# A row write of a direction in four transfers instead of six, and a signal for each of the two kinds of rows

## Chip, cores and metric

One core of one Trainium2 chip. The metric is the device time of one execution of the whole program, in microseconds; the kernel runs one program on that core.

## The reference

The model is a small vision tower on 32 images of 96 x 96: patches to tokens, a state-space layer, a mixture of 8 experts (top 2), then a second layer with a two-directional Mamba block and another top-2 mixture. There are 38 tokens an image and 192 features. The change lies in how the two scans get their inputs. They compute, cut to the core:

```python
# layer 0, per token: features Dm=192, states N=16
dA = jnp.exp(a[:, None, :] * dt[None, :, None])
cur = u_t[:, :, None] * (b[:, None, :] * dt[None, :, None])
state = (dlt[:, :, None] * state + (1.0 - dlt[:, :, None]) * cur) * dA
y = jnp.sum(state * c[:, None, :], axis=2) + u_t * D_param

# layer 1, for each of two directions: features DI=192, states NS=16
dt = jax.nn.softplus(dt @ dt_W + dt_b)
dA = jnp.exp(dt_t[:, :, None] * A)
h = dA * h + (dt_t * u_t)[:, :, None] * B_t[:, None, :]
y = (h * C_t[:, None, :]).sum(-1)
```

## The kernel before, in words

The 32 images are worked on in 4 groups of 8 images, T = 304 tokens each. Features lie on the partitions: the first 128 in one piece, the last 64 packed, so that a row block of 128 partitions and PK = 304 + 152 columns holds all of them: columns 0 to 303 are features 0 to 127, columns 304 to 455 hold features 128 to 191, with the first half of the tokens on partitions 0 to 63 and the second half on partitions 64 to 127.

A scan wants another layout: 16 states x 8 features on the partitions. So each direction of a group writes two kinds of rows to DRAM (rows_d, 2 x 2 x 192 x 304): kind 0 is DL, the steps (in the first pass the deltas), kind 1 is WV, the steps times the input. Each of the 12 steps of a scan (QSTEPS, 16 features each) reads its share of both kinds back, each feature's row broadcast to 16 partitions, into one of 4 slots of a ring (dA and BB, fill_slot, line 470).

The program has three parts. The first pass (layer 0's scan, line 505 on for SyncE) goes through the groups; the experts follow (lines 507 to 551); the second pass does, for each group, direction 0 (part_a) and direction 1 (part_b) of the Mamba block, with the tail of the group before and the input of the group after written by hand between the 12 steps of each part. Each engine's order is written out: its function for a part runs n = 0 to 11 and places each piece of work at a given n.

What the prediction's steps touch:

- SyncE issues all the row transfers. `write_first_rows` (line 462) writes a group's rows in the first pass, six transfers, after the signal P.w_ready. `write_rows` (line 579) does it in the second pass, six transfers, after Q.w_ready, which is signalled by the memset at line 1258. For direction 1 it is called ahead of the read of step 11 of direction 0; for direction 0 of the next group, after the last read of direction 1. `read_rows` (line 590) waits until the scan four steps before has freed the slot. `rows_there` (line 587) waits until all the writes of a direction have landed. After the write for the next group stands `read_gates` (line 601), three reads of the gates of the group before, and only then `rows_there` and the reads of direction 0 of the next group.
- VectorE's `steps` (line 1243) makes the rows: five operations on 128 x 456 numbers (lines 1249 to 1254), each of which waits for the one before through the signal PREP.chain, then a memset of one token of each image of DL to RESTART (1e16), so that the scan starts anew there. It is placed at n = 6 of part_a for direction 1 and at n = 7 of part_b for direction 0 of the next group. `direction_step` (line 1189) multiplies the next step's BB by B (line 1186) and scans (line 1200). `gated_output` (line 1260) takes the sum of the direction before, at n = 1.
- ScalarE takes the exponential of the dA rows two steps ahead (`q_decay`, line 864), and waits for Q.w_ready before it overwrites the buffer LZ (line 859). In the first pass `delta` (line 899) waits for the writes of the group before.
- GpSimd multiplies the scan's result by C (line 725), and the mixture's inputs by the gates (line 733).
- TensorE sums over the states (line 1641), takes the gated output (`direction_out`, line 1625), and does the products of the mixture, spread over the steps around the turn from one group to the next; line 1514 is the helper that issues all its products. `add_mixture` (line 1425) on VectorE waits for them.

Of the kernel before, what the change touches and what calls it, by code (L numbers as in the profile page):

```python
# [9 lines left out]
T = IMG * SEQ  # L10
# [95 lines left out]
def vit_tower(nc, x_p, c128a, c64a, c128, c64, ex_m, ex_r, ex_b, out_m, out_r):  # L106
    fp32, bf16, i32, u32 = mybir.dt.float32, mybir.dt.bfloat16, mybir.dt.int32, mybir.dt.uint32
    ALU, ACT, AX = mybir.AluOpType, mybir.ActivationFunctionType, mybir.AxisListType
    with ExitStack() as ctx:
# [211 lines left out]
        P.w_ready, Q.w_ready, base_ready = sig("p_w_ready", 1), sig("q_w_ready", 2), sig("base_ready", 1)  # L321

# [5 lines left out]
        P.rows_written, rows_written = both_passes("rows_written", 96)  # L328
# [10 lines left out]
        PREP.chain, NORM.chain = sig("prep_chain", 10), sig("norm_chain", 2)  # L339
# [108 lines left out]
        def _(sp):  # L448
# [12 lines left out]

            def write_first_rows(p):

                sp.wait_ge(P.w_ready.sem, P.w_ready.after(p, 1))
                for kind, x in enumerate((P.DL, P.WV)):
                    sp.dma_start(rows_d[p % 2, kind, 0:DM, :], x[:, 0:T]).then_inc(P.rows_written.sem, 16)
                    sp.dma_start(rows_d[p % 2, kind, DM:D, 0:HALF], x[0:DR, T:PK]).then_inc(P.rows_written.sem, 16)
                    sp.dma_start(rows_d[p % 2, kind, DM:D, HALF:T], x[DR:128, T:PK]).then_inc(P.rows_written.sem, 16)
# [17 lines left out]
            def first(s, p, m):  # L486
                if s is not None:
                    sp.wait_ge(P.rows_written.sem, P.rows_written.after(s, 96))
                for c in range(QSTEPS):
                    if c == 5:  # L490
                        if m is not None:
                            sp.wait_ge(scan_out.sem, scan_out.after(m, 1))
                            sp.dma_start(h_md[m], M.Hm[:, :]).then_inc(h_stored.sem, 16)
                            sp.dma_start(h_rd[m], M.Hr[:, :]).then_inc(h_stored.sem, 16)
                        if follows(p) is not None:
                            sp.wait_ge(tok_mm.sem, tok_mm.after(p, 2))
                            sp.dma_start(xp[:, :, :], x_p[p + 1]).then_inc(s_x, 16)
                    if c == QSTEPS - 1 and p is not None:
                        write_first_rows(p)
                    if s is not None:  # L500
                        read_first_rows(s, c)
                    if s == 0 and c >= SLOTS:
                        sp.dma_start(zeros[:, c - SLOTS, :], ZERO).then_inc(s_zero, 16)
# [75 lines left out]
            def write_rows(g, k):  # L579

                sp.wait_ge(Q.w_ready.sem, Q.w_ready.after(g, k + 1))
                for kind, x in enumerate((DIRS[k].DL, DIRS[k].WV)):
                    sp.dma_start(rows_d[k, kind, 0:DM, :], x[:, 0:T]).then_inc(rows_written.sem, 16)
                    sp.dma_start(rows_d[k, kind, DM:D, 0:HALF], x[0:DR, T:PK]).then_inc(rows_written.sem, 16)
                    sp.dma_start(rows_d[k, kind, DM:D, HALF:T], x[DR:128, T:PK]).then_inc(rows_written.sem, 16)

            def rows_there(g, k):
                sp.wait_ge(rows_written.sem, rows_written.after(g, 96 * (k + 1)))
# [169 lines left out]
        def _(act):  # L758
# [140 lines left out]
            def delta(s, p):  # L899
                act.wait_ge(delta_mm.sem, delta_mm.after(p, 1))  # L900
                if s is not None:
                    act.wait_ge(P.rows_written.sem, P.rows_written.after(s, 96))
# [139 lines left out]
        def _(dve):  # L1042
# [200 lines left out]
            def steps(g, k):  # L1243

                s = DIRS[k]
                links[PREP] = 5 * k
# [7 lines left out]
                link(PREP, g, nc.vector.tensor_tensor(s.WV[:, :], s.DL[:, :], s.UP[:, :], ALU.mult))  # L1254
                assert links[PREP] == 5 * k + 5, links[PREP]

                first = slice(SEQ - 1, SEQ) if k == 1 else slice(0, 1)
                nc.vector.memset(seqs(s.DL[:, :])[:, :, first], RESTART).then_inc(Q.w_ready.sem, 1)
# [808 lines left out]
```

## Time and profile before

| | |
|---|---|
| median of 3 runs | 1063.36 us (1062.62 to 1064.8) |
| the profiled execution | 1062.3 us |
| its span on the core | 1060.6 us |
| mean granted TensorE clock | 0.803 of full speed |
| TensorE (PE) busy | 737.7 us, 70% of the span |
| VectorE (DVE) | 653.2 us, 62% |
| ScalarE (ACT) | 430.1 us, 41% |
| GpSimd (POOL) | 441.6 us, 42% |
| queue of SyncE (q1), share of 16 DMA engines | 54.8% |
| rows_d to dA, 144 transfers of 304 KB | 3.8 us median to landing |
| rows_d to BB, 144 transfers of 304 KB | 4.4 us median to landing |

The profile is one execution; its own time stands beside its span, and the three timed runs are others. PEld is TensorE's loading of weights, SPq the queue of SyncE's DMA issues. A span of a DMA issue in the queue is the time in which the issue occupies the queue, not the transfer. In the timelines an entry in square brackets is the time for which the engine stood idle before, and what ended it. "DMA share" is the mean busy share of the 16 DMA engines, where 1.00 is all of them busy.

### The profile page before, as it was taken

Reading aid. Unit: us, or ns where it says so; the run is one execution under the profiler, and the core shown is the slowest. Engines: PE = TensorE matmul, PEld = TensorE weight load, DVE = VectorE, ACT = ScalarE, POOL = GpSimd, SP = SyncE. Lnnn points to the kernel's source line nnn. Section 1 sums busy time; section 2 is a strip of 40 time slices with the busy share of each in tenths; the row PEclk is TensorE's granted clock in tenths of the full one; section 3 lists DMA queues with packets and bytes.
Section 4 is the critical chain, followed back from the end, with each engine's and each line's share of the span. In section 5 each row is a group of like instructions: output and inputs, shape, how many; then the busy total and the mean of one; then the engine's idle time right before and its main releaser. Section 6 shows DMA issues by size and latency. Waiting matters only on the chain.

```text
span 1060.6 us, 10874 instructions
## 1 busy us (share of the span) xinstructions
PE 737.7 (70%) x3286; PEld 564.8 (53%) x3286; DVE 653.2 (62%) x954; ACT 430.1 (41%) x863; POOL 441.6 (42%) x304
## 2 busy tenths in 40 slices
PE   6968778576555459999645558656697687775845
PEld 5635556354334349999624346534475456553623
DVE  3197988778796402112111797889868987799220
ACT  3547265265220213333223547365626462644120
POOL 0065655755867121111210454464367336544403
PEclk8989789688566569999958679789878787976857
DMA  9486644344441079999501867666586657577002
GB/s 341 122 288 237 197 118 110 101 118 116 118 96 48 7 203 297 299 291 290 157 22 38 224 172 195 162 177 174 143 203 171 156 142 230 134 192 188 17 15 65
DMA packets 79725, 168.98 MB, mean 159 GB/s; under 512 B 12068, under 2 KB 30256, under 8 KB 78912
## 3 DMA queue, kind: packets, MB, share of 16 engines
q1 hardware_dynamic: 75184, 161.90, 54.8%
q0 software_dynamic: 4496, 6.55, 2.1%
q8 instruction: 20, 0.33, 0.1%
q14 instruction: 25, 0.20, 0.1%
HBM read 148.37 MB, written 20.01 MB: 159 GB/s over the span
## 4 chain that ended last, share of the span: by engine, by line
PE 37%; DVE 18%; issue 14%; POOL 10%; DMA 9%; ACT 9%; SPq 2%; DVEq 0%; POOLq 0%; ACTq 0%
PE PS L1514 36%; DVE ST L1200 5%; DMA BB<-rows_d 4%; POOL dA L657 3%; POOL slots_d L671 3%; DVE BB L1186 2%; POOL PR L666 2%; DMA WXR<-ex_r 2%; POOL PR L725 1%; DMA CR<-c 1%; DMA keep_d<-KEEP 1%; ACT L819 1%; ACT L888 1%; ACT dA L869 1%; ACT aP L888 1%
## 5 line engine op out<-in xcount | busy, mean ns | idle before, releaser
L1514 PE MATMUL PS<-PR,CM 128*128 128x304 f32 (+1 forms) x768 | 224.1, 439 | 133.0 <-POOL PR L725 74.6
L1514 PEld LDWEIGHTS PS<-PR,CM 128*128 128x128 f32 x768 | 153.7, 238 | 189.5 <-POOL PR L725 93.1
L1200 DVE TENSOR_TENSOR_SCAN ST<-dA,BB 128x608 f32<-128x608 f32 x96 | 160.0, 1671 | 3.0 <-POOL PR L725 2.9
L869 ACT ACTIVATE dA<-dA,negA 128x304 f32<-128x304 f32 x192 | 93.7, 539 | 144.1 <-DMA BB<-rows_d 144.0
L725 POOL TENSOR_TENSOR PR<-ST,q_V 128x608 f32<-128x608 f32 x48 | 74.9, 1561 | 135.0 <-DVE ST L1200 120.2
L725 POOL TENSOR_TENSOR PR<-ST,p_V 128x608 f32<-128x608 f32 x48 | 84.0, 1753 | 106.2 <-DVE ST L1200 98.6
L657 POOL TENSOR_TENSOR dA<-dA,aP 128x608 f32<-128x608 f32 x48 | 88.8, 1851 | 58.9 <-ACT aP L888 52.6
L1177 DVE TENSOR_TENSOR_SCAN ST<-dA,BB 128x608 f32<-128x608 f32 x48 | 99.8, 2080 | 19.0 <-issue 16.2
L1186 DVE TENSOR_TENSOR BB<-BB,PS 128x608 f32<-128x608 f32 x96 | 74.0, 773 | 31.8 <-DMA BB<-rows_d 31.1
L965 ACT ACTIVATE HID<-PS,WX 128x128 f32<-128x128 f32 x162 | 47.8, 365 | 103.0 <-PE PS L1514 103.0
L701 POOL DMA_DIRECT2D outs_d<-xp x27 | 14.7, 545 | 130.6 <-DVE xp L1373 130.6
L1514 PE MATMUL PS<-XT,WX 128*128 128x128 f32 x324 | 64.7, 282 | 3.0 <-DMA WXR<-ex_r 1.5
L1514 PE MATMUL PS<-XT,WXR 128*128 128x128 f32 x324 | 63.6, 278 | 0.0
L1514 PE MATMUL PS<-WX,CM 128*128 128x304 f32 x192 | 54.8, 436 | 9.5 <-POOL WX L733 9.5
L1365 DVE COPY XT<-PS 128x128 f32<-128x128 f32 x27 | 7.9, 292 | 85.7 <-PE PS L1775 85.7
L1514 PE MATMUL PS<-WX,HID 128*128 128x192 f32 x324 | 57.4, 326 | 0.5 <-issue 0.5
L1172 DVE TENSOR_TENSOR BB<-BB,aP 128x608 f32<-128x608 f32 x48 | 54.8, 1141 | 1.2 <-ACT aP L888 1.2
L666 POOL TENSOR_TENSOR PR<-ST,q_V 128x608 f32<-128x608 f32 x24 | 37.2, 1549 | 43.1 <-DVE ST L1177 35.1
L666 POOL TENSOR_TENSOR PR<-ST,p_V 128x608 f32<-128x608 f32 x24 | 36.7, 1530 | 44.1 <-DVE ST L1177 31.7
L1514 PEld LDWEIGHTS PS<-XT,WX 128*128 128x128 f32 x324 | 50.8, 195 | 5.9 <-issue 3.6
L1514 PEld LDWEIGHTS PS<-WX,HID 128*128 128x128 f32 x324 | 52.2, 190 | 0.8 <-issue 0.8
L1514 PEld LDWEIGHTS PS<-WX,CM 128*128 128x128 f32 x192 | 38.2, 201 | 24.1 <-POOL WX L733 10.4
(333 smaller groups left out, 1419.1 us busy)
## 6 DMA issues: line engine op xcount, KB each, us to landing
dA<-rows_d SPq DMA_DIRECT2D x144, 304.0 KB, 3.8
BB<-rows_d SPq DMA_DIRECT2D x144, 304.0 KB, 4.4
WX<-ex_m SPq DMA_DIRECT2D x27, 576.0 KB, 4.7
WX<-ex_m SPq DMA_DIRECT2D x27, 387.0 KB, 4.1
slots_d<-WXR SPq DMA_DIRECT2D x8, 960.0 KB, 7.5
WXR<-ex_r SPq DMA_DIRECT2D x27, 192.0 KB, 5.1
WX<-gates_d SPq DMA_DIRECT2D x4, 1216.0 KB, 6.3
CM<-c SPq DMA_DIRECT2D x1, 4430.0 KB, 19.9
```

The source lines that it names most:

```text
L657: nc.gpsimd.tensor_tensor(dAq[:, slot], dAq[:, slot], EXq[:, c % EXPS], ALU.mult).then_inc(ap_ready.sem, 1)
L666: nc.gpsimd.tensor_tensor(PRq[:, c % 2], STq[:, c % 2], CS[s % 2][:, :].unsqueeze(1).broadcast_to([128, QB, T]), ALU.mult).then_inc(P.prod ...
L671: pool.indirect_dma_start(slots_d[:, :], bass.IndirectOffsetOnAxis(slot_u[:, t, k:k + 1], 0), XTOK[0:TW, t, :], None).then_inc(scattered.s ...
L725: nc.gpsimd.tensor_tensor(PRq[:, c % 2], STq[:, c % 2], DIRS[k].Cw.unsqueeze(1).broadcast_to([128, QB, T]), ALU.mult).then_inc(q_product.s ...
L869: last = nc.scalar.activation(dAq[:, slot, i, :], dAq[:, slot, i, :], ACT.Exp, scale=negA[:, j:j + 1])
L888: last = nc.scalar.activation(EXq[:, c % EXPS, i, :], AS[g % 2][:, :], ACT.Exp, scale=neg_dtq[:, j:j + 1])
L965: last = nc.scalar.activation(HX[:, p, f, :], PS[:, WIDE_BANK + 2 * p + h, j * 128:(j + 1) * 128], ACT.Gelu, bias=WX[:, p, FFN + f:FFN + f ...
L1172: nc.vector.tensor_tensor(BBq[:, slot], BBq[:, slot], EXq[:, c % EXPS], ALU.mult).then_inc(b_times_a.sem, 1)
L1177: nc.vector.tensor_tensor_scan(flat(STq[:, c % 2], False), flat(dAq[:, slot], False), flat(BBq[:, slot], False), 0.0, ALU.mult, ALU.add).t ...
L1186: nc.vector.tensor_tensor(BBq[:, slot], BBq[:, slot], PS[:, BW_BANK[k], 0:T].unsqueeze(1).broadcast_to([128, QB, T]), ALU.mult).then_inc(b ...
L1200: nc.vector.tensor_tensor_scan(flat(STq[:, c % 2], back), flat(dAq[:, slot], back), flat(BBq[:, slot], back), 0.0, ALU.mult, ALU.add).then ...
L1514: return nc.tensor.matmul(out, lhsT, rhs, start=first, stop=last)
```

## The change

The two transfers of the last 64 features become one, whose DRAM side is a view with the halves as its outermost dimension. A direction's rows then take four transfers, and the counts of the signals go from 96 to 64. In the second pass the rows WV are written first, after Q.w_ready, which is now signalled by the product at line 1254; the rows DL follow after a new signal, steps_ready, which the memset gives. VectorE waits for Q.w_ready itself in place of the fifth link of PREP.chain. In the first pass the order of the kinds and the signal stay.

```diff
+        steps_ready = sig("steps_ready", 2)
...
-        P.rows_written, rows_written = both_passes("rows_written", 96)
+        P.rows_written, rows_written = both_passes("rows_written", 64)
...
-        PREP.chain, NORM.chain = sig("prep_chain", 10), sig("norm_chain", 2)
+        PREP.chain, NORM.chain = sig("prep_chain", 8), sig("norm_chain", 2)
...
+            def write_both(k, kind, x, signal):
+
+                sp.dma_start(rows_d[k, kind, 0:DM, :], x[:, 0:T]).then_inc(signal.sem, 16)
+                rest = rows_d[k, kind, DM:D, :].rearrange("r (h t) -> h r t", h=2)
+                sp.dma_start(rest, x[:, T:PK]).then_inc(signal.sem, 16)
+
             def write_first_rows(p):
 
                 sp.wait_ge(P.w_ready.sem, P.w_ready.after(p, 1))
                 for kind, x in enumerate((P.DL, P.WV)):
-                    sp.dma_start(rows_d[p % 2, kind, 0:DM, :], x[:, 0:T]).then_inc(P.rows_written.sem, 16)
-                    sp.dma_start(rows_d[p % 2, kind, DM:D, 0:HALF], x[0:DR, T:PK]).then_inc(P.rows_written.sem, 16)
-                    sp.dma_start(rows_d[p % 2, kind, DM:D, HALF:T], x[DR:128, T:PK]).then_inc(P.rows_written.sem, 16)
+                    write_both(p % 2, kind, x, P.rows_written)
...
             def write_rows(g, k):
 
                 sp.wait_ge(Q.w_ready.sem, Q.w_ready.after(g, k + 1))
-                for kind, x in enumerate((DIRS[k].DL, DIRS[k].WV)):
-                    sp.dma_start(rows_d[k, kind, 0:DM, :], x[:, 0:T]).then_inc(rows_written.sem, 16)
-                    sp.dma_start(rows_d[k, kind, DM:D, 0:HALF], x[0:DR, T:PK]).then_inc(rows_written.sem, 16)
-                    sp.dma_start(rows_d[k, kind, DM:D, HALF:T], x[DR:128, T:PK]).then_inc(rows_written.sem, 16)
+                write_both(k, 1, DIRS[k].WV, rows_written)
+                sp.wait_ge(steps_ready.sem, steps_ready.after(g, k + 1))
+                write_both(k, 0, DIRS[k].DL, rows_written)
 
             def rows_there(g, k):
-                sp.wait_ge(rows_written.sem, rows_written.after(g, 96 * (k + 1)))
+                sp.wait_ge(rows_written.sem, rows_written.after(g, 64 * (k + 1)))
...
-                links[PREP] = 5 * k
+                links[PREP] = 4 * k
...
-                link(PREP, g, nc.vector.tensor_tensor(s.WV[:, :], s.DL[:, :], s.UP[:, :], ALU.mult))
-                assert links[PREP] == 5 * k + 5, links[PREP]
+                nc.vector.tensor_tensor(s.WV[:, :], s.DL[:, :], s.UP[:, :], ALU.mult).then_inc(Q.w_ready.sem, 1)
+                dve.wait_ge(Q.w_ready.sem, Q.w_ready.after(g, k + 1))
+                assert links[PREP] == 4 * k + 4, links[PREP]
 
                 first = slice(SEQ - 1, SEQ) if k == 1 else slice(0, 1)
-                nc.vector.memset(seqs(s.DL[:, :])[:, :, first], RESTART).then_inc(Q.w_ready.sem, 1)
+                nc.vector.memset(seqs(s.DL[:, :])[:, :, first], RESTART).then_inc(steps_ready.sem, 1)
```

The two other places where 96 is waited for, the reads of the first pass and ScalarE's `delta`, wait for 64.

## Rows read from the trace of the kernel before

**Rows 1.** The page: share of the chain that ended last, by engine
```profile
PE 37%; DVE 18%; issue 14%; POOL 10%; DMA 9%; ACT 9%; SPq 2%; DVEq 0%; POOLq 0%; ACTq 0%
```

**Rows 2.** Waits of all engines: engine line waited for: us, times, longest
```profile
DVE BB L1186 <- DMA BB<-rows_d: 31.1, 11, 9.7
```

**Rows 3.** Timeline of SP's queue, group 0, direction 0: start us, us, engine, line
```profile
575.33 0.33 SPq L583 DMA_DIRECT2D rows_d<-q_DL  x1
575.70 0.47 SPq L584 DMA_DIRECT2D rows_d<-q_DL  x1
576.22 0.60 SPq L585 DMA_DIRECT2D rows_d<-q_DL  x1
576.86 0.58 SPq L583 DMA_DIRECT2D rows_d<-q_WV  x1
577.48 0.45 SPq L584 DMA_DIRECT2D rows_d<-q_WV  x1
577.97 0.60 SPq L585 DMA_DIRECT2D rows_d<-q_WV  x1
579.93 0.57 SPq L477 DMA_DIRECT2D dA<-rows_d  x1
```

**Rows 4.** DMA view, 575 to 581 us (six row writes alone)
```profile
DMA packets 608, 0.47 MB, mean 78 GB/s; under 512 B 96, under 2 KB 608, under 8 KB 608
```

**Rows 5.** DMA view, 1029 to 1032.3 us (one write of 8 rows alone)
```profile
DMA packets 16, 0.01 MB, mean 3 GB/s; under 512 B 8, under 2 KB 16, under 8 KB 16
...
q1 hardware_dynamic: 16, 0.01, 1.5%
```

**Rows 6.** Windows: us, busy PE PEld DVE ACT POOL, clock, DMA share, GB/s
```profile
576.00:576.60 0.60, 0.00 (x0) 0.00 (x0) 0.00 (x0) 0.00 (x0) 0.00 (x0) 1.00 0.68 249
...
578.50:579.10 0.60, 0.00 (x0) 0.00 (x0) 0.00 (x0) 0.00 (x0) 0.00 (x0) 0.83 0.26 65
579.10:579.90 0.80, 0.00 (x0) 0.00 (x0) 0.00 (x0) 0.00 (x0) 0.00 (x0) 0.50 0.19 49
```

**Rows 7.** Timeline of DVE: first BB product of each direction 0 that waited
```profile
585.04 0.79 DVE L1186 TENSOR_TENSOR BB<-BB,PS 128x608 f32<-128x608 f32 x1 [9.74 <-DMA BB<-rows_d]
...
677.90 0.79 DVE L1186 TENSOR_TENSOR BB<-BB,PS 128x608 f32<-128x608 f32 x1 [1.47 <-DMA BB<-rows_d]
...
778.78 0.79 DVE L1186 TENSOR_TENSOR BB<-BB,PS 128x608 f32<-128x608 f32 x1 [5.58 <-DMA BB<-rows_d]
...
890.03 0.79 DVE L1186 TENSOR_TENSOR BB<-BB,PS 128x608 f32<-128x608 f32 x1 [5.47 <-DMA BB<-rows_d]
```

**Rows 8.** Timelines of ACT and DVE, group 0, step 11 of direction 0
```profile
624.34 0.99 ACT L869 ACTIVATE dA<-dA,negA 128x304 f32<-128x304 f32 x2 [8.46 <-DMA BB<-rows_d]
...
625.48 0.76 DVE L1186 TENSOR_TENSOR BB<-BB,PS 128x608 f32<-128x608 f32 x1
```

**Rows 9.** Timelines of DVE and PE: gated output, then PE's use, groups 1 to 3
```profile
684.99 0.31 DVE L1270 TENSOR_TENSOR HID<-p_TM,aP 64x152 f32<-64x152 f32 x1
...
687.10 0.68 PE L1514 MATMUL PS<-p_WV,CM 128*96 128x304 f32 x2
...
790.75 1.49 DVE L1270 TENSOR_TENSOR HID<-p_TM,aP 64x152 f32<-64x152 f32 x1
...
792.86 0.68 PE L1514 MATMUL PS<-p_WV,CM 128*96 128x304 f32 x2
...
900.29 1.50 DVE L1270 TENSOR_TENSOR HID<-p_TM,aP 64x152 f32<-64x152 f32 x1
...
903.15 0.67 PE L1514 MATMUL PS<-p_WV,CM 128*96 128x304 f32 x2
```

**Rows 10.** Timeline of DVE, group 2: the mixture's wait for PE
```profile
808.29 0.47 DVE L1428 TENSOR_TENSOR Om<-q_Hm,PS 128x304 f32<-128x304 f32 x1 [4.25 <-issue]
```

**Rows 11.** Timeline of DVE, first pass: its first scan
```profile
53.44 2.61 DVE L1177 TENSOR_TENSOR_SCAN ST<-dA,BB 128x608 f32<-128x608 f32 x1 [1.43 <-POOL dA L657]
```

More of the change, by code:

```diff
@@ L487, in first @@
                 if s is not None:
-                    sp.wait_ge(P.rows_written.sem, P.rows_written.after(s, 96))
+                    sp.wait_ge(P.rows_written.sem, P.rows_written.after(s, 64))
                 for c in range(QSTEPS):
@@ L901, in delta @@
                 if s is not None:
-                    act.wait_ge(P.rows_written.sem, P.rows_written.after(s, 96))
+                    act.wait_ge(P.rows_written.sem, P.rows_written.after(s, 64))
                 nc.scalar.activation(P.DL[:, 0:T], PS[:, MEAN_BANK, 0:T], ACT.Sigmoid, bias=cm("d_b2", 0, 1))
```

## The prediction, made before the changed kernel was run

> **What bounds the kernel now.** I read the page first. Its chain that ended last gives PE 37%, DVE 18%, DMA 9% and SP's queue 2% [rows 1]: no engine bounds all of it, so a row write counts only where the next engine has no slack. The writes are made twelve times: four in the first pass, eight in the second.
>
> SP's queue shows one set. Six issues start at 575.33, 575.70, 576.22, 576.86, 577.48 and 577.97, and the first read of these rows starts at 579.93, so a set takes 4.60 us from its first issue to the reads [rows 3]. The third and sixth issues take 0.60 each. Of the 4.60, 2.64 is issuing up to the last issue's start, and 1.96 runs from there to the release.
>
> Next, DVE: which of its waits are for these reads? In the second pass it reaches the first products of direction 0 early and idles 9.74 (group 0), 1.47 (group 1), 5.58 (group 2) and 5.47 us (group 3) [rows 7]. In direction 1 the write is issued while DVE still has scans to do.
>
> Last, what PE does with DVE's work. In groups 1 to 3 the gated output (line 1270) of the direction before ends at 685.30, 792.24 and 901.79, and PE takes it up at 687.10, 792.86 and 903.15 [rows 9]. The queue of PE was busy until then, so DVE is 1.80, 0.62 and 1.36 us ahead. Later in group 2 DVE itself stands 4.25 us before line 1428, which waits for PE's products of the mixture (the row has "issue" as the releaser) [rows 10]. PE bounds these stretches, and time that DVE wins at the transitions is mostly not seen at the end.
>
> **The change, part by part.**
>
> Fewer issues. A set becomes main rows, rest rows, main, rest. With the gaps of 0.04 between issues and the row's 0.60 as the most that the joined issue takes, the fourth starts 0.33 + 0.04 + 0.60 + 0.04 + 0.58 + 0.04 = 1.63 us after the first, against 2.64: 1.0 us less [rows 3]. If the joined issue takes 0.45, it is 0.15 less still.
>
> Order and signals. W·V's product ends at 575.16 and the memset starts at 575.24 for 0.07 [rows 2]; the first issue now follows the memset at 575.33. With the product first, it starts about 0.13 us earlier. The memset is over before SP has issued two writes, so the new wait on the steps costs nothing there. Behind that wait stand the two writes of the steps, then the last read of the running direction; they are later by nothing as long as the memset follows the product directly, which it does. DVE's links stay five: the product's own signal is waited on in place of the fifth. ACT's wait on it before line 860 gets its signal 0.1 us sooner; harmless. In the first pass the order stays, only the joining acts.
>
> The joined transfer. This is the term that no row of before shows. Its SBUF side is 128 rows of 152 numbers, its DRAM side is written (h t), that is 2 by 64 by 152. What spreads a transfer over the 16 DMA engines? Packets under 512 B are here the completions: six writes of 64 or 128 rows leave 96 of them, 16 for each [rows 4], but the write of the 8 gate rows leaves 8 [rows 5]. So a transfer goes to as many engines as its outermost length allows, 8 for 8. The new DRAM side's outermost length is 2. I take two engines, the value that the 8-row write points to; the other end is 16, if the 128 rows of the SBUF side decide.
>
> The Trainium skill has a rule for this ("DMA: Bandwidth & Descriptors", section "Why a DMA increments its semaphore by 16 and not by 1"): the number of engines is the largest up to 16 that divides the slowest length of both sides. By that rule it is 2; the 8 completions above agree, and no row of before shows a case where the two sides differ.
>
> Price of it. Two stretches with nothing but 608-byte packets hold the fifth and sixth writes, 128 packets and 32 completions: (0.60 x 0.26 + 0.80 x 0.19) x 16 = 4.93 engine-us [rows 6], 38 ns a packet with the completions in it. The gate write's 8 packets and 8 completions took 1.5% of 3.3 us on 16 engines, 0.79 engine-us, 99 ns a pair [rows 5]; a 1216-byte packet takes at most 0.60 x 0.68 x 16 / 128 = 51 ns [rows 6], so a completion takes about 48, and the 608-byte packet (4.93 - 32 x 0.048) / 128 = 27 ns. A joined write has 2 completions instead of 32, so I take 30 ns, near the lower figure. It puts 64 packets on each of two engines: 1.92 us (1.73 to 2.43).
>
> The chain on these two engines: the first joined issue starts 0.37 after the first issue, and the data of a small write starts about 1.1 us after its issue (577.97 against the stretch from 579.10), so its data runs from 1.4 to 3.3. Then 8 packets of the main rows, 0.4, then the second joined write, 1.92, then about 0.2 to the release: 5.84 us, 5.71 with the earlier start, against 4.60. The set is released 1.1 us later, not earlier (0.75 later at 27 ns, 2.15 at 38). With 16 engines it is 1.15 earlier.
>
> Where that lands:
> - Group 0, direction 0: everything idles behind the reads [rows 7]: +1.1 in full.
> - Group 0, direction 1: the read of step 11 is issued behind the writes on the same two engines. It lands by 624.34, and DVE, busy without a gap, needs it at 625.48 [rows 8]: 1.14 of slack, 0 at 1.1, +1.0 at 2.15. The other three sets of direction 1 have several us of scans as cover: 0. If that cover went, each would cost what the first one does.
> - Groups 1, 2, 3, direction 0: 1.1 less the 1.80, 0.62 and 1.36 of slack [rows 9]: 0, +0.5, 0 (0.35, 1.5 and 0.8 at 2.15).
> - First pass: the first scan waits for the POOL product of the decays, that is for ACT's work and not for rows [rows 11]: 0. The other three sets have step 7's to 9's work as cover: 0.
>
> Sum: +1.6 us (at 27 ns: 0.75 + 0.15 = +0.9; at 38 ns: 2.15 + 1.0 + 0.35 + 1.5 + 0.8 = +5.8). The profiled execution took 1062.3 us (span 1060.6), so 1063.9 against itself. The median of the three runs, 1063.36, is 1.06 above it, so I give 1065.0. About 0.2%, 2.1 us, is what a measurement of this kernel can tell from no change: this forecast lies just inside.
>
> **Rivals.**
> 1. All 16 engines take the joined write. For it: the SBUF side has 128 rows, and every write of 64 or more rows got 16 [rows 4]. Against it: the 8-row write. Each release is then 1.15 earlier. Group 0 takes it whole. In groups 1 to 3 PE has no use for it [rows 9, 10]. Result -1.2: 1062.2.
> 2. The same, but with PE's slack being only the shadow of the late rows, so that each of the four transitions wins its 1.15: -4.6, 1058.8. Against it: the 4.25 us that DVE waits for PE after such a transition [rows 10].
> 3. Slower. Two engines carry the writes at 38 ns or worse, and the gate rows' and scan rows' reads queue behind them on those two, so that every read waits for its slowest sixteenth. The place is the transition to direction 0 of groups 2 and 3, where gate reads follow the writes and DVE already idles 5.5 us [rows 7]. It decides from a delay of about 1.4 us on, where the slacks of 0.62, 1.36 and 1.14 are gone, and each further us costs up to four. At 38 ns: +5.8, 1069.2.
> 4. The reordering does nothing that shows: W·V's signal comes only 0.13 before the old one, since the memset is 0.07 long [rows 2]. This holds in every case above, and is worth 0.13 us at most where the set is exposed.
>
> **How the numbers follow.** Two engines: 0.80, split into the forecast (delay of 0.7 to 1.4 us) 0.48 and rival 3, 0.32, as 30 ns is a reading between 27 and 38 and a long run on one engine has no row here. Sixteen engines: rival 1 0.14, rival 2 0.06. Faster by over 0.2%: rival 2 and a little of rival 1, 0.07. Slower by over 0.2%: rival 3 and a tenth of the forecast, 0.37. Within: 0.56. The range runs from a little under rival 1 to rival 3's end: 1061.6 to 1069.3.
>
> **What would show it.** In the changed kernel, the DMA view around the first set of the second pass: 36 completions under 512 B (16 + 2 + 16 + 2) would prove two engines, 64 would prove rival 1. SP's queue: first issue to first read 5.7 us rather than 4.60 (or 3.6). DVE's four waits of rows 7 longer by 1 us (or shorter). PE's take-up of the gated output in group 2 directly behind line 1270, with an idle time, would show that the slack is used up. I am wrong if SP's issues themselves get longer because two engines' queues are full, or if the joined issue costs well over 0.60.

## The result and the profile after

| | before | after |
|---|---|---|
| median | 1064.08 us (4 runs) | 1077.82 us (4 runs) |
| ratio to before, 95% interval | | 1.0122 (1.0075 to 1.017), that is +13.0 us (8.0 to 18.1) |
| profiled execution, span | 1062.3, 1060.6 us | 1077.3, 1075.6 us |

The change makes the kernel slower by 1.2%. The forecast was 1065.0 us, the range ended at 1069.3, and the side that was given 0.37 came out.

The page of the changed kernel, the lines that changed (line numbers of the changed kernel are 4 to 5 higher in this part of the file):

```profile
PE 749.0 (70%) x3286; PEld 568.1 (53%) x3286; DVE 653.1 (61%) x954; ACT 430.2 (40%) x863; POOL 439.5 (41%) x304
...
DMA packets 79005, 168.97 MB, mean 157 GB/s; under 512 B 11348, under 2 KB 29536, under 8 KB 78192
...
q1 hardware_dynamic: 74464, 161.89, 54.3%
...
PE 38%; DVE 16%; issue 15%; POOL 12%; DMA 9%; ACT 9%; SPq 2%; DVEq 0%; POOLq 0%; ACTq 0%
...
L1190 DVE TENSOR_TENSOR BB<-BB,PS 128x608 f32<-128x608 f32 x96 | 73.9, 773 | 40.8 <-DMA BB<-rows_d 40.3
```

No engine has more to do: VectorE, ScalarE and GpSimd are busy as long as before, within 2.1 us; PE is busy 11 us longer with the same 3286 matmuls. What grew is idling behind reads of the rows: VectorE's before its BB product from 31.1 to 40.3 us. The packets under 512 B went from 12068 to 11348, 720 fewer, 60 in each of the 12 sets: 96 completions to a set became 36 = 16 + 2 + 16 + 2. Each joined write was carried by two engines.

The queue of SP at the set that stands in [rows 3]:

```profile
578.07 0.33 SPq L465 DMA_DIRECT2D rows_d<-q_WV  x1
578.43 0.58 SPq L467 DMA_DIRECT2D rows_d<-q_WV  x1
579.06 0.46 SPq L465 DMA_DIRECT2D rows_d<-q_DL  x1
579.56 0.53 SPq L467 DMA_DIRECT2D rows_d<-q_DL  x1
585.54 0.59 SPq L482 DMA_DIRECT2D dA<-rows_d  x1
```

The last issue comes 1.15 us sooner than with six, about as expected: the fourth starts 1.49 us after the first (the sixth 2.64 before). But from the last issue to the first read there are now 5.98 us for 1.96, and the set takes 7.47 us for 4.60. Windows of the same stretch (window, its length, five engines busy, PE clock, busy share of the 16 DMA engines, GB/s):

```profile
578.60:579.60 1.00, 0.06 (x1) 0.00 (x0) 0.00 (x0) 0.00 (x0) 0.00 (x0) 1.00 0.45 156
579.60:580.60 1.00, 0.00 (x0) 0.00 (x0) 0.00 (x0) 0.00 (x0) 0.00 (x0) 1.00 0.28 49
580.60:582.00 1.40, 0.00 (x0) 0.00 (x0) 0.00 (x0) 0.00 (x0) 0.00 (x0) 1.00 0.43 129
582.00:583.00 1.00, 0.00 (x0) 0.00 (x0) 0.00 (x0) 0.00 (x0) 0.00 (x0) 1.00 0.10 8
583.00:585.10 2.10, 0.00 (x0) 0.00 (x0) 0.00 (x0) 0.00 (x0) 0.00 (x0) 0.58 0.12 36
585.10:585.60 0.50, 0.00 (x0) 0.00 (x0) 0.00 (x0) 0.00 (x0) 0.00 (x0) 0.50 0.00 0
```

The last two rows with data are the two engines alone: a share of 0.12 of 16 is 1.9 engines. From 583.0 to 585.1 they move 36 GB/s, 76 KB, which is nearly all of the second joined write: 64 packets on each engine in 2.1 us, 33 ns a packet. What ran ahead of it can be told from three DMA views, of 581.5 to 581.8, 581.8 to 582.0 and 582.0 to 583.0 us:

```profile
DMA packets 19, 0.01 MB, mean 45 GB/s; under 512 B 2, under 2 KB 19, under 8 KB 19
...
DMA packets 7, 0.01 MB, mean 43 GB/s; under 512 B 0, under 2 KB 7, under 8 KB 7
...
DMA packets 10, 0.01 MB, mean 8 GB/s; under 512 B 1, under 2 KB 10, under 8 KB 10
```

The two packets under 512 B in the first view are the completions of the first joined write, so it was done 3.4 to 3.7 us after the first issue. The seven packets of the second view carry 1.2 KB each (43 GB/s for 0.2 us), so they are rows of the wide DL write: the 8 rows that fell to each of the two engines come behind the first joined write, although the other 14 engines were done with theirs by 581.2. In the third view, nine data packets move 8 KB. That is about four of these wide rows and the first five packets of the second joined write, and 0.10 of 16, 1.6 engines, count as busy for it: some 160 ns a packet. So the wide rows of the two engines, for which the prediction had 0.4 us, last from 581.6 to about 582.9. After the last packet (584.9) about 0.6 us pass to the release.

What it does downstream, in VectorE's timeline, the first product of direction 0 in groups 0 to 3:

```profile
590.76 0.79 DVE L1190 TENSOR_TENSOR BB<-BB,PS 128x608 f32<-128x608 f32 x1 [12.58 <-DMA BB<-rows_d]
...
685.56 0.79 DVE L1190 TENSOR_TENSOR BB<-BB,PS 128x608 f32<-128x608 f32 x1 [2.64 <-DMA BB<-rows_d]
...
791.69 0.79 DVE L1190 TENSOR_TENSOR BB<-BB,PS 128x608 f32<-128x608 f32 x1 [8.49 <-DMA BB<-rows_d]
...
903.86 0.79 DVE L1190 TENSOR_TENSOR BB<-BB,PS 128x608 f32<-128x608 f32 x1 [8.52 <-DMA BB<-rows_d]
```

Against [rows 7] each of these waits is longer, by 2.84 (group 0), 2.91 (group 2) and 3.05 us (group 3). In group 1 the row of [rows 7] is the second product; the first one did not wait for a DMA at all:

```profile
675.68 0.76 DVE L1186 TENSOR_TENSOR BB<-BB,PS 128x608 f32<-128x608 f32 x1
```

A better scale is the time from a set's first issue to this first product. Before, it is 9.71, 9.73, 15.39 and 15.28 us in groups 0 to 3; after, 12.69, 12.60, 18.45 and 18.48. The four add up to 12.1 us of lateness, and the kernel is 13.0 us slower. So the loss looks like these four sets, each handed on whole. That was an inference from one pair of traces; the runs below test it, and for groups 2 and 3 they do not bear out that the late rows hand it on.

### The profile page after: what moved, and what is told of

It is laid out like the page before. It is cut to its first block, busy times and chain, and to the rows that moved or that the text cites. A ratio compares the mean times of both kernels' runs of the same rounds, so it can differ in the third digit from the quotient of the medians.

```text
span 1075.6 us, 10850 instructions
## 1 busy us (share of the span) xinstructions
PE 749.0 (70%) x3286; PEld 568.1 (53%) x3286; DVE 653.1 (61%) x954; ACT 430.2 (40%) x863; POOL 439.5 (41%) x304
## 2 busy tenths in 40 slices
DMA packets 79005, 168.97 MB, mean 157 GB/s; under 512 B 11348, under 2 KB 29536, under 8 KB 78192
## 4 chain that ended last, share of the span: by engine, by line
PE 38%; DVE 16%; issue 15%; POOL 12%; DMA 9%; ACT 9%; SPq 2%; DVEq 0%; POOLq 0%; ACTq 0%
PE PS L1519 38%; DVE ST L1204 4%; DMA BB<-rows_d 3%; POOL dA L661 3%; POOL slots_d L675 3%; POOL PR L670 3%; DVE BB L1190 2%; POOL PR L729 2%; DMA xp<-outs_d,slot_u 1%; POOL xp L715 1%; DMA WXR<-ex_r 1%; DMA CR<-c 1%; ACT aP L892 1%; DMA keep_d<-KEEP 1%; ACT L823 1%
## 5 line engine op out<-in xcount | busy, mean ns | idle before, releaser
L1519 PE MATMUL PS<-PR,CM 128*128 128x304 f32 (+1 forms) x768 | 227.8, 443 | 132.8 <-POOL PR L729 76.5
L1190 DVE TENSOR_TENSOR BB<-BB,PS 128x608 f32<-128x608 f32 x96 | 73.9, 773 | 40.8 <-DMA BB<-rows_d 40.3
L1519 PE MATMUL PS<-WX,CM 128*128 128x304 f32 x192 | 57.0, 449 | 15.3 <-POOL WX L737 15.3
L1519 PEld LDWEIGHTS PS<-WX,CM 128*128 128x128 f32 x192 | 38.6, 204 | 31.1 <-POOL WX L737 17.6
```

Of the source, the lines that this page charges most:

```text
L1190: nc.vector.tensor_tensor(BBq[:, slot], BBq[:, slot], PS[:, BW_BANK[k], 0:T].unsqueeze(1).broadcast_to([128, QB, T]), ALU.mult).then_inc(b ...
L1519: return nc.tensor.matmul(out, lhsT, rhs, start=first, stop=last)
```

## The experiments

Theory A: the joined writes are the cost, because two engines carry them one after the other. Rival B: the new order and the added wait. Then: which sets, why those, and does the lateness alone do it. The stretch in the table is from a set's first issue to the first read of its rows, in groups 0 to 3 of the second pass, direction 0. Each time stands beside the ratio to the kernel before on the same chip, since that kernel's own median moved between 1064.1 and 1066.2 us from one group of runs to the next.

| run | what is joined, order | stretch, us | median, us | ratio (95%) |
|---|---|---|---|---|
| before | none, DL first | 4.60, 4.60, 5.38, 5.41 | | 1 |
| after | both, WV first | 7.47, 7.44, 7.48, 7.41 | 1077.8 | 1.0122 (1.0075 to 1.017) |
| e1_split | none, WV first, two signals | 4.61, 4.60, 5.41, 5.32 | 1064.4 | 0.9997 (0.997 to 1.0024) |
| e2_join_only | both, DL first, one signal | 7.38, 7.38, 8.13, 8.12 | 1084.2 | 1.0174 (1.0123 to 1.0224) |
| e12_joined_last | both, wide writes first | 6.97, 6.99, 6.96, 6.96 | 1076.5 | 1.0101 (1.0052 to 1.0149) |
| e6_wv_joined | WV alone, first | 4.91, 4.87, 4.92, 4.92 | 1064.9 | 1.0006 (0.9978 to 1.0033) |
| e9_dl_joined | DL alone, last | 6.03, 5.99, 6.87, 6.88 | 1071.6 | 1.0066 (1.0042 to 1.009) |
| e3_first_joined | both, first pass only | 4.60 (group 0) | 1064.9 | 0.9986 (0.9961 to 1.0011) |
| e7_k1_joined | both, direction 1 only | 4.62, 4.61, 5.37, 5.44 | 1063.9 | 1.0002 (0.9977 to 1.0027) |
| e8_k0_joined | both, direction 0 only | 7.49, 7.45, 7.45, 7.47 | 1079.0 | 1.0135 (1.0084 to 1.0185) |
| e5_g0_joined | both, direction 0, group 0 | 7.46, 4.61, 5.39, 5.35 | 1065.8 | 1.0013 (0.9985 to 1.004) |
| e13_early_groups | both, direction 0, groups 0, 1 | 7.51, 7.41, 5.33, 5.40 | 1070.2 | 1.0046 (1.0022 to 1.0071) |
| e14_late_groups | both, direction 0, groups 2, 3 | 4.61, 4.61, 7.49, 7.47 | 1075.5 | 1.0075 (1.0049 to 1.0101) |
| e10_late_reads | none, WV first, a 64-byte write before the reads | 5.66, 5.67, 12.20, 12.09 | 1069.1 | 1.0027 (1.0001 to 1.0053) |
| e11_kinds_together | DL and WV in one transfer, three to a set | 3.29, 3.26, 3.80, 3.84 | 1063.6 | 0.9977 (0.9949 to 1.0005) |

**The joining or the order?**

e1_split:

```
-                rest = rows_d[k, kind, DM:D, :].rearrange("r (h t) -> h r t", h=2)
-                sp.dma_start(rest, x[:, T:PK]).then_inc(signal.sem, 16)
+                sp.dma_start(rows_d[k, kind, DM:D, 0:HALF], x[0:DR, T:PK]).then_inc(signal.sem, 16)
+                sp.dma_start(rows_d[k, kind, DM:D, HALF:T], x[DR:128, T:PK]).then_inc(signal.sem, 16)
```

> Only the order and the two signals of the change are kept (WV rows first, DL behind its own signal); each pair of halves goes in two writes of 64 rows again, six transfers to a set. Theory A, the joined writes are the cost (they are carried by two DMA engines, 2 completions each where the split pair had 32, and these last 1.9 us a write and more): 96 small completions a set come back, the stretch from first issue to first read at the exposed set of the second pass falls from 7.47 us back to about 4.6, and the time to that of the kernel before less a few tenths: 1063.5 us, within 1 us. Rival B, the order and the added wait on VectorE and SP are the cost: the stretch is short but the time stays near 1077. Rival C, half and half: about 1070.

e2_join_only is the kernel before with the same two lines joined instead, and 64 for 96 in the waits.

> The kernel before with the joined write alone: one signal, DL rows first, four transfers to a set. Theory A: all of the cost is here, about 1077 us (1075 to 1079), with 36 completions under 512 bytes in the exposed set and first issue to first read near 7 us. Rival B: about 1064. The order can matter in one way that A allows: the last transfer is then the joined WV write, as it was the joined DL write, so no difference is expected from that.

Theory A holds. Without the joined writes the time is that of before, the completions are 12068 again, and the stretch is 4.61. With them alone the loss is there, even a larger one by the medians: 1084.2 lies above the 1075 to 1079 that were expected, though the intervals of the two ratios overlap. The order that was to win 0.1 us does nothing that a measurement sees while the writes are split. While they are joined it may help: in groups 2 and 3 the stretch is 8.13 and 8.12 us with DL first, 7.48 and 7.41 with WV first.

**One joined write or two?**

e6_wv_joined joins only where `kind == 1`, e9_dl_joined only where `kind == 0`; the other kind has its two writes.

> The changed kernel with the WV rows' halves joined and the DL rows' halves split, in all sets: five transfers, 66 completions under 512 bytes and fewer. If the cost is the packets of a joined write on two engines alone, the WV one, issued a microsecond ahead of the end, is mostly hidden: first issue to first read 5 us, time about 1065. If it is the low stretch of about 1 us between the two joined writes (10 packets from 582 to 583 us), which the first joined write makes by itself, the split DL writes wait behind it on the two engines: stretch 6 to 6.5 us, time about 1070.

> The mirror of the run with only the WV writes joined: the WV halves split, the DL halves joined, in all sets, so the one joined write is the last of the set. If two joined writes have to follow one another on the same two engines for the loss: stretch at the exposed set 5 to 5.5 us and the time within 2 us of 1064.4, 1066 us. If it is enough that the last write of a set is a joined one: stretch near 7 us, about 1076.

The joined WV write alone makes the stretch 0.3 us longer in the early groups and 0.4 to 0.5 shorter in the late ones, and costs nothing in the time that can be measured: its packets on two engines run beside the issues and the DL writes. The joined DL write alone, being last, makes the stretch 1.4 to 1.6 us longer, which is about the 1.9 us of its packets less the issue saved, and costs 7.0 us (4.5 to 9.6 by the ratio). That is more than the two that were expected; the stretch of 6.0 lies between the two expectations. Both together make it 2.9 in groups 0 and 1. So they are not independent: 0.3 + 1.4 gives 1.7. By the three views above the rest comes where the wide rows and the second joined write queue behind the first joined write on the same two engines; no run separates that queueing from the slow packets.

e12_joined_last asks what the slow packets belong to. Its edit to the kernel before is the order of the transfers:

```
+                for kind, x in enumerate((dl, wv)):
+                    sp.dma_start(rows_d[k, kind, 0:DM, :], x[:, 0:T]).then_inc(signal.sem, 16)
+                for kind, x in enumerate((dl, wv)):
+                    rest = rows_d[k, kind, DM:D, :].rearrange("r (h t) -> h r t", h=2)
+                    sp.dma_start(rest, x[:, T:PK]).then_inc(signal.sem, 16)
```

> The kernel before with joined halves and its one signal, but both wide writes first and both joined ones last, so that no wide write shares the two engines with a joined one. If the slow packets of 582 to 583 us come from a joined write having to follow another (or from its own start): stretch 7 to 7.5 us at the exposed set and 1078 to 1084 us. If they come from the wide write that stands between the two: stretch 6 us and about 1071.

The stretch is 6.97 us, 0.5 less than in the changed kernel, and the time 1076.5 us, a little less; both lie just under the range of the first expectation and far from the second. The wide write between the two is thus not the main cause of the long stretch. The view of all DMA engines from 575.2 to 582.3 us in 40 slices:

```profile
DMA  0000069789601111111011111111111111110000
GB/s 0 0 0 0 0 253 397 261 301 336 206 0 27 34 31 45 48 7 24 10 45 45 45 45 38 45 41 45 41 34 38 38 38 38 34 41 3 0 0 0
DMA packets 548, 0.47 MB, mean 66 GB/s; under 512 B 36, under 2 KB 548, under 8 KB 548
```

All 16 engines are done with the wide writes by the eleventh slice. The two joined writes then take 24 of the 40 slices, 4.3 us, at 45 to 48 GB/s at best (45 is 22.5 on each engine, 27 ns a packet), 34 to 41 in the second half, and with a dip to 7 to 24 for half a microsecond. Here the dip comes inside the first joined write, with the wide writes over. In e9_dl_joined one stands inside the only joined write of the set (8 packets from 579.7 to 580.1 us), so it needs no second joined write either; in e6_wv_joined there is none. What makes it was not found.

**Which sets?**

e3_first_joined, e7_k1_joined, e8_k0_joined and e5_g0_joined are the changed kernel with split writes but for the sets named (`in_first`; `k == 1`; `k == 0`; `(g, k) == (0, 0)`).

> The changed kernel with joined writes in the first pass only (4 of its 12 sets), split ones in the 8 sets of the second pass. Theory A from the two traces: the steps of the first pass came 0.3 to 1.1 us later and the experts' start 1.4 us later, so 1064 plus 1 to 1.5, 1065.3 us; the second pass starts that much later and loses no more. Rival: the drift of 2.9 us that stood at the start of the second pass comes wholly from the first pass's writes: 1067 us.

> Joined writes only in the four sets of the second direction of the second pass, which SP issues ahead of the last read of a direction and needs some 4 us later. Theory that the exposed sets cost the time: at most 1 us, 1065 us. Rival, that they do not stay covered (the drift grew by 1.1 us after this set in group 0): four times 1 us, 1068 us.

> Joined writes only in the four sets of the first direction of the second pass; at groups 1 to 3 the reads of the gates and of the first rows stand behind them in SP's queue. Theory that the loss is in these: 1064.4 plus 2.8 at group 0 and 2 to 3.6 at each of the others, 1074 to 1076 us. Rival, that the two directions' sets cost alike: 1070 us.

> Joined writes only in one of the 12 sets, the first direction of group 0 in the second pass, where SP and VectorE wait for the landing; order and signals as changed. Stretch from first issue to first read 7.4 us there. If the delay is handed on one to one: 1064.4 plus 2.8, 1067.2 us. If later stages catch it up (the drift that stood in the changed kernel came from other places): 1065 or less.

Eight of the twelve sets, those of the first pass and of direction 1, cost nothing that can be measured (both intervals lie around 1). The expected +1 us for the first pass did not come. This also tells against a reading of the traces: in the changed one the second pass began almost 3 us later than before (first issue at 578.07 for 575.33), which looked like a loss in the first pass and the experts; e3 has the same joined writes there and its median is not above before's. A difference of that size between two single executions is no evidence. In the 15 traces that first issue of the second pass stands anywhere from 573.6 to 579.2 us. All of the loss that can be measured is in the four sets of direction 0: 1.0135 for them alone, 1.0122 for the whole change (the 1079.0 us are more than the 1074 to 1076 that were expected). Group 0's alone gives +1.4 us (-1.6 to +4.3), an interval that holds both nothing and the whole 3 us, so this run settles nothing.

**Lateness, or load on the two engines?**

e10_late_reads takes e1_split and puts one tiny round trip between the landing of the rows and their first read:

```
+            def idle_trip(g):
+                sp.dma_start(nowhere_d[:, :], CR[0:1, 0:16]).then_inc(trip, 16)
+                sp.wait_ge(trip, 16 * (g + 1))
...
                 rows_there(g, 0)
+                idle_trip(g)
```

> No joined write at all (the run with split halves, changed order and two signals), but SP, after the rows of a first direction have landed in the second pass, sends one 64-byte write and waits for it before it reads the rows: the first read comes later by one such round trip, some 2 us, four times, 8 us in all, with no load on any DMA engine. Joined sets made the same stretches longer by 2.9, 2.8, 2.1 and 2.1 us (9.9 in all) and cost 13 to 14 us. Theory that the lateness of the first read alone sets the cost, with the same gearing of 1.3 to 1.4: 1064.4 plus 11, 1075 us. Rival, that the joined writes also hold up the reads of the gates and of the rows behind them on the two engines, and that this makes the part over 9.9: 1064.4 plus 8 or less, 1072 us or under.

The round trip was not what was planned. In group 0 it is short:

```profile
580.95 0.24 SPq L618 DMA_DIRECT2D nowhere_d<-CR  x1
582.00 0.57 SPq L484 DMA_DIRECT2D dA<-rows_d  x1
```

In groups 2 and 3 the same 64 bytes stand behind the reads of the gates:

```profile
774.33 0.49 SPq L618 DMA_DIRECT2D nowhere_d<-CR  x1
781.22 0.53 SPq L484 DMA_DIRECT2D dA<-rows_d  x1
```

1.05 us alone, 6.89 us behind the gates' reads. The first read is issued 12.2 us after the set's first issue there, 4.7 later than in the changed kernel, and yet the run costs only +2.9 us (0.1 to 5.6), 1069.1 us. That is on the rival's side (1072 or under), although the delays were not the 2 us that both expectations assumed. When the first read is *issued* is not the scale, since in groups 2 and 3 it stands behind the gates' data anyway. When VectorE gets its rows is nearer to it, but not enough. First issue to first product is 10.49, 10.67, 17.73 and 17.51 us, against 9.44, 9.87, 15.03 and 15.05 in e1: 7.0 us of lateness in all, 5.2 of them in groups 2 and 3. On the same scale, against e1, the changed kernel has 12.8. That 7.0 cost 2.9 (0.1 to 5.6), while 12.8 cost 13.0 (8.0 to 18.1), leaves room for a second path. The reads of the gates are one: GpSimd's first product with the gates, in group 2, before and after:

```profile
776.07 1.47 POOL L733 TENSOR_TENSOR WX<-WX,q_Xm 128x608 f32<-128x608 f32 x1 [1.60 <-DMA WX<-gates_d]
```

```profile
789.83 1.46 POOL L737 TENSOR_TENSOR WX<-WX,q_Xm 128x608 f32<-128x608 f32 x1 [5.37 <-DMA WX<-gates_d]
```

Counted from the set's first issue that is 12.68 us before and 16.59 after, 3.9 later, more than the rows, although the first of these reads is issued 1.2 us sooner (2.04 us after the set's first issue for 3.28); with e10 it is 12.54, no later at all. Its consumer is PE, with its idle time, before and after:

```profile
778.73 2.99 PE L1514 MATMUL PS<-WX,CM 128*128 128x304 f32 x8
```

```profile
791.34 4.00 PE L1519 MATMUL PS<-WX,CM 128*128 128x304 f32 x8 [2.74 <-POOL WX L737]
```

Before, PE goes to the mixture without an idle time; after, it stands 2.74 us behind GpSimd, which stands behind the gates, which stand behind the joined writes. In the DMA view of 773 to 781 us the engines move 100 to 440 GB/s from 776.6 us on, which is mostly the gates' reads, while the set's own writes are released only at 780.7: the other engines already carry their shares of the gates, so the lateness is put down to the two shares that wait.

Which of the two paths hands the loss on in groups 2 and 3 can be followed in the traces. The times in us count from the set's first issue. "Gated" is the end of VectorE's gated output of the direction before (line 1270 before), "PE" is where TensorE takes it up, and "mixture" is where VectorE, having waited for TensorE, takes the mixture (line 1428 before). Each cell has group 2, then group 3.

| run | first product, VectorE | gates product, GpSimd | gated | PE | mixture |
|---|---|---|---|---|---|
| before | 15.39, 15.28 | 12.68, 13.20 | 28.85, 27.04 | 29.47, 28.40 | 44.90, 43.84 |
| e1_split | 15.03, 15.05 | 12.59, 12.67 | 27.57, 26.85 | 28.46, 29.52 | 43.90, 44.95 |
| e10_late_reads (rows late, gates not) | 17.73, 17.51 | 12.54, 12.50 | 29.87, 29.60 | 29.92, 29.66 | 45.43, 45.17 |
| after (rows and gates late) | 18.45, 18.48 | 16.59, 16.48 | 30.11, 30.17 | 33.24, 33.14 | 48.68, 48.57 |
| e14_late_groups (the same) | 18.52, 18.31 | 16.66, 16.30 | 30.11, 29.93 | 33.32, 33.59 | 48.76, 49.03 |

The six runs with neither late (before, e1, e3, e5, e7, e13) reach the mixture after 43.0 to 45.0 us, 44.2 in the mean. With the rows alone 2.5 to 2.7 us late it is 45.3, 1.1 later; with the gates late too it is 48.6 to 49.0, some 4.5 later. Two times 4.5 fits the +8.0 us (5.2 to 10.8) that the last pair of runs gives for groups 2 and 3. The lines for group 2, after the change and in e10, show the two ways:

```profile
801.85 1.50 DVE L1275 TENSOR_TENSOR HID<-p_TM,aP 64x152 f32<-64x152 f32 x1
806.48 0.68 PE L1519 MATMUL PS<-p_WV,CM 128*96 128x304 f32 x2
821.92 0.47 DVE L1433 TENSOR_TENSOR Om<-q_Hm,PS 128x304 f32<-128x304 f32 x1 [5.89 <-PE PS L1519]
```

```profile
797.39 1.50 DVE L1283 TENSOR_TENSOR HID<-p_TM,aP 64x152 f32<-64x152 f32 x1
798.94 0.75 PE L1527 MATMUL PS<-p_WV,CM 128*96 128x304 f32 x2 [1.03 <-DVE HID L1283]
814.45 0.47 DVE L1441 TENSOR_TENSOR Om<-q_Hm,PS 128x304 f32<-128x304 f32 x1 [3.76 <-PE PS L1527]
```

With late rows alone PE stands 1.03 us behind VectorE, and VectorE's own wait for the mixture shrinks to 3.76 us (4.51 in e1): most of the lateness is absorbed. In the changed kernel VectorE is 3.13 us ahead of PE, more than the 0.62 of before. So in groups 2 and 3 most of the loss comes by the gates, GpSimd and PE, and not by the rows. In group 1, which has no reads of gates behind its writes, PE does stand behind VectorE:

```profile
695.51 0.90 PE L1519 MATMUL PS<-p_WV,CM 128*96 128x304 f32 x2 [2.42 <-DVE HID L1275]
```

**Do all four hand it on?** The last pair divides the four sets.

> Joined writes only in the first direction's sets of groups 0 and 1 of the second pass (2 of 12 sets). In the changed kernel VectorE's first product behind these sets began 3.3 and about 2.4 us later after the set's first issue than with split writes. If lateness arrives whole at the end at every group: 1064.4 plus 5.7, 1070 us. If the early groups absorb most of theirs, as the run with group 0's set alone hints (1065.8): 1066 us.

> The other two: joined writes only in the first direction's sets of groups 2 and 3, with the gates' reads behind them; VectorE's first product was 3.4 us later at each. If lateness arrives whole: 1064.4 plus 6.8, 1071 us, and the two runs together make up the 13 to 14 us of the whole. If these two carry more than their lateness, because the gates' product on GpSimd also starts 4 us later: 1074 us.

The lateness against e1 measured in these runs is 2.9 and 2.4 us in groups 0 and 1 of e13, 5.2 in all, and 3.5 and 3.3 in groups 2 and 3 of e14, 6.8 in all. The ratios give +4.9 us (2.3 to 7.6) and +8.0 (5.2 to 10.8), together 12.9, as the whole change has 13.0. The early pair came out as "arrives whole" has it; the late pair's median of 1075.5 us is above both of its expectations, its ratio between them. Both halves cost about their lateness, but in the late pair that is no sign that the rows carry it: by the table above rows that were 2.6 us late alone moved the mixture by about 1 us. The intervals are too wide to tell 8.0 from 6.8.

**A version with fewer transfers that keeps 16 engines.**

e11_kinds_together starts from the kernel before. DL and WV share a buffer, and one transfer takes both kinds of the same features, so that features are outermost on both sides:

```
+            s.DW = sb(name + "_DW", [128, 2, PK])
+            s.DL, s.WV = s.DW[:, 0, :], s.DW[:, 1, :]
...
+                for part, rows, cols in ((x[:, :, 0:T], slice(0, DM), slice(0, T)),
+                                         (x[0:DR, :, T:PK], slice(DM, D), slice(0, HALF)),
+                                         (x[DR:128, :, T:PK], slice(DM, D), slice(HALF, T))):
+                    sp.dma_start(rows_d[k, :, rows, cols].rearrange("a r t -> r a t"), part).then_inc(signal.sem, 16)
```

> Another way to fewer transfers: DL and WV of a direction lie side by side in one buffer, and each transfer takes both kinds; three to a set (the first 128 features, then either half of the last 64), with the features outermost on both sides, so that 16 engines should carry each. Completions per set 48, all three by 16. The set's last issue comes 1.5 us earlier than with six; 456 KB at the 344 GB/s of the wide writes are 1.3 us. Stretch from first issue to first read 3.3 to 3.7 us for 4.60, about 1.1 us less at each of the four sets; with the gearing of 1.3 seen with the joined writes 1064.4 less 5, 1059 us. Rival, that the data and not the issues set the stretch with 16 engines: no change, 1064.

The stretch was sized right. SP's queue at the exposed set:

```profile
577.29 1.72 SPq L467 DMA_DIRECT2D rows_d<-q_DW  x3
580.58 0.55 SPq L481 DMA_DIRECT2D dA<-rows_d  x1
```

3.29 us for 4.60, and the DMA view from 577.0 to 580.6 us:

```profile
DMA packets 560, 0.47 MB, mean 130 GB/s; under 512 B 48, under 2 KB 560, under 8 KB 560
```

48 completions, 16 a transfer. First issue to first product falls to 8.34, 9.73 (no wait for rows there), 13.46 and 13.57 us, 1.4, 0, 1.9 and 1.7 less than before, 5.0 in all. The time: median 1063.6 us beside 1065.6 of the kernel before in the same group, ratio 0.9977 (0.9949 to 1.0005), that is -2.4 us (-5.4 to +0.5). Probably a gain of about a fifth of a per cent, not a proven one; the 5 us that were expected are at the interval's edge.

## Why the prediction was wrong

- **Two engines for a joined write: right.** 36 completions a set, as named. The Trainium skill's rule ("DMA: Bandwidth & Descriptors", section "Why a DMA increments its semaphore by 16 and not by 1"), the largest number up to 16 that divides the slowest length of both sides, holds here in the case that no row of before had: 128 on the SBUF side, 2 on the DRAM side, two engines. The features-outermost form in e11 gives 16.
- **Issues: right.** The fourth issue starts 1.49 us after the first for 1.63, with 0.58 and 0.53 for the joined ones. The first issue follows the product by 0.04 us for 0.17, the 0.13 that was named. (The product's and the memset's times, 575.16 and 575.24, are those of the trace, but the rows that the prediction names for them do not show them.)
- **Price of a packet, 30 ns (27 to 38): right for the stream, the sum of the set wrong.** The stream runs at 27 to 33 ns. The set was put at 5.84 us and takes 7.47. The step that failed is "its data runs from 1.4 to 3.3. Then 8 packets of the main rows, 0.4, then the second joined write, 1.92, then about 0.2 to the release". The first joined write ended 3.4 to 3.7 us after the first issue instead of 3.3. The term that was missed most is the wide rows behind it on the two engines, "8 packets of the main rows, 0.4": they lasted from 581.6 to about 582.9 us, some 1.3, with packets of about 160 ns at their end. The second joined write was done 2.0 to 2.1 us later for 1.92, and the release took about 0.6 for 0.2. Together +2.9 us instead of +1.1. The upper bound of 2.15 was made of packets at 38 ns alone and did not reach it. This is the larger part of the miss: with 2.9 put through the rest of the working as it stands, group 0 gives 2.9, the slacks leave 1.1, 2.3 and 1.5 in groups 1 to 3, and step 11 of group 0 adds 1.7: 9.5 us for the 1.6 of the forecast.
- **Landing: wrong too.** "1.1 less the 1.80, 0.62 and 1.36 of slack: 0, +0.5, 0". The runs show +4.9 for the pair of groups 0 and 1 and +8.0 for groups 2 and 3. For groups 2 and 3 the forecast followed the wrong path. It charged them for late rows on VectorE alone, against VectorE's lead over PE at the gated output [rows 9]. That lead was not used up: it is 3.13 and 2.97 us in the changed kernel. The gates' reads, queued behind the same writes, came 3.9 us later, GpSimd's product with them, and PE stood 2.74 us behind it; the forecast's sum has no term for this; only rival 3 names these reads. VectorE's wait for the mixture, 4.25 us [rows 10], which should have paid for late rows, grew to 5.89 us, because PE was late too. In group 1 the path was right: PE's idle time of 2.42 us behind VectorE shows the slack used up, and by the same working a set that is 2.9 us late leaves 1.1 there. At step 11 of group 0, where 1.7 us would have been charged, VectorE's product, at 632.54 in the changed kernel, waits for no DMA; e7 costs +0.2 us (-2.4 to +2.9).
- **First pass and direction 1: nothing, right** (e3, e7: ratios 0.9986 and 1.0002), and so was the guess that the reordering does nothing that shows (e1: 0.9997). The intervals leave room for nearly 3 us.
- **Rival 3 had the mechanism:** two engines, with gate and scan reads behind the writes, in groups 2 and 3. It was given 0.32 and priced 1069.2 us, because it stood on the same bound of 38 ns and the same slacks. The packets did not take its 38 ns, and the slacks did not go in groups 2 and 3.
- The prediction took group 1's 1.47 us in [rows 7] for the wait of the first product. It is the second; the first had none. So group 1 looked half covered. In the changed kernel its first product waits 2.64 us.

## What to carry to other kernels

Before joining transfers to save issues, look at the outermost length of both sides: a DRAM view written (h t) with h = 2 outermost ran on two engines here, and whatever came behind it on those two, wide rows, a second such write and reads, waited there while the others stood free. Saving two issues, 1.15 us, made the rows 2.9 us later. To save issues, put things side by side under a long outermost dimension, as with both kinds of a direction. And before a lead of one engine over another is taken for slack, follow every reader that is queued behind the same transfers: here the gates' reads reached the engine that was to give the slack.

## What was not expected of the hardware

- Two engines that stream 608-byte packets at 27 to 33 ns each have stretches in which a packet takes about 160 ns: 10 packets in the microsecond from 582 to 583, with 1.6 engines busy. Such dips, half as long, stand in e12 after the wide writes are over and in e9 inside the only joined write. Open.
- The wide rows of the two engines ran behind the joined write that was issued before them, 1.7 us after the last of the other 14 engines had ended (581.2 against about 582.9).
- Costs of transfers on few engines do not add: 0.3 us of stretch for the first joined write alone, 1.4 for the last alone, 2.9 for both (groups 0 and 1).
- A write of 64 bytes takes 1.05 us from issue to the release of the next instruction when the queue is empty, and 6.89 us behind the three reads of the gates in the same queue.
